# A sandwich block on one core: mean-free Wo with its bias as a product, a maximum over two PSUM banks, and a bank ring by last use

## The reference

```
x = x + layernorm(attention(layernorm(x)))      # RoPE, causal softmax, ctx @ Wo + b_out
x = x + layernorm(ffn(layernorm(x)))
ffn: scores = sigmoid(xt @ w_router.T); the two best, weights divided by their sum
     silu(xt @ wg.T) * (xt @ wu.T) @ wd.T of each chosen expert, weighted and summed,
     plus the same of both shared experts
layernorm(x) = (x - mean) / sqrt(var + 1e-5)     # over the last axis, no scale, no shift
```

## Time and profile before

| | us |
|---|---|
| median of 3 runs | 760.34 (759.79 to 762.09) |
| the profiled execution | 760.28 |
| its span, first to last instruction | 757.8 |
| PE busy | 705.5 (93%) |
| DVE busy | 605.7 (80%) |
| ACT busy | 431.8 (57%) |

### The profile page before, as it was taken

One profiled execution on the slowest core, in us unless ns is written; L12 is line 12 of the kernel. 1 busy time (PEld: TensorE's weight loads), 2 busy tenths in 40 slices (PEclk: granted clock), 3 DMA queues, 4 the chain that ended last, 5 costly groups with the idle time before them and its releaser, 6 DMA issues. The chain is left out here.

```text
span 757.8 us, 15818 instructions
## 1 busy us (share of the span) xinstructions
PE 705.5 (93%) x6002; PEld 564.7 (75%) x6002; DVE 605.7 (80%) x1364; ACT 431.8 (57%) x729; POOL 314.7 (42%) x444
## 2 busy tenths in 40 slices
PE   4779999999999998979998999999999999999994
PEld 2335555555555555768888999999999999988884
DVE  4998999999998885565866888888878878738885
ACT  2436765666667576334244777777776777632230
POOL 4113354454444455100223455445445543048854
PEclk9989999999999999989999999999999999999998
DMA  8000000000000000000124676776667676513311
GB/s 278 1 3 4 4 3 10 16 10 11 10 11 10 16 11 15 15 8 1 43 91 174 208 236 217 223 236 216 239 217 233 221 215 202 163 56 90 91 57 55
DMA packets 29131, 74.31 MB, mean 98 GB/s; under 512 B 4609, under 2 KB 18305, under 8 KB 29057
## 3 DMA queue, kind: packets, MB, share of 16 engines
q0 software_dynamic: 12208, 55.45, 22.6%
q1 hardware_dynamic: 16432, 17.20, 6.9%
q10 hardware_dynamic: 416, 0.66, 0.3%
HBM read 62.68 MB, written 10.22 MB: 96 GB/s over the span
## 5 line engine op out<-in xcount | busy, mean ns | idle before, releaser
L984 DVE TENSOR_TENSOR HF<-SS,PS 128x256 f32<-128x256 f32 (+1 forms) x155 | 75.9, 490 | 98.2 <-ACT SS L732 57.0
L732 ACT ACTIVATE SS<-PS 128x256 f32<-128x256 f32 (+1 forms) x155 | 68.2, 440 | 116.7 <-PE PS L396 112.2
L396 PE MATMUL PS<-XGH,WH 128*128 128x256 f32 x460 | 129.6, 282 | 2.8 <-DVE WL L1084 2.8
L396 PE MATMUL PS<-XGL,WH 128*128 128x256 f32 x460 | 129.3, 281 | 0.0
L396 PE MATMUL PS<-XGH,WL 128*128 128x256 f32 x460 | 129.3, 281 | 0.0
L821 DVE TENSOR_REDUCE NM<-PS 128x2 f32<-128x512 f32 (+1 forms) x192 | 122.6, 682 | 7.6 <-PE PS L396 6.6
L1084 DVE TENSOR_TENSOR WL<-RAW,WH 128x768 fp32r<-128x768 f32 x125 | 120.2, 963 | 3.5 <-ACT WH L659 2.8
L396 PE MATMUL PS<-WH,HH 128*128 128x256 f32 x390 | 112.4, 288 | 0.9 <-DVE ACC L995 0.8
L659 ACT ACTIVATE HH<-HF 128x256 fp32r<-128x256 f32 (+1 forms) x155 | 72.1, 465 | 71.4 <-DVE HF L984 64.1
L396 PE MATMUL PS<-WL,HH 128*128 128x256 f32 x390 | 110.4, 283 | 0.0
L396 PE MATMUL PS<-WH,HL 128*128 128x256 f32 x390 | 110.4, 283 | 0.0
(11 more groups left out here) (167 smaller groups left out, 1460.2 us busy)
## 6 DMA issues: line engine op xcount, KB each, us to landing
ys<-YO SPq DMA_DIRECT2D x23, 256.0 KB
RAW<-in_wsh SPq DMA_DIRECT2D x4, 768.0 KB, 6.5
X<-in_x SPq DMA_DIRECT2D x8, 256.0 KB, 5.3
xn<-YY SPq DMA_DIRECT2D x16, 128.0 KB, 1.7
out<-X SPq DMA_DIRECT2D x16, 128.0 KB
QT<-NMT SPq DMA_DIRECT2D x96, 4.0 KB
RAW<-in_wsh SPq DMA_DIRECT2D x2, 384.0 KB, 6.1
XG<-xn,XIDX POOLq DMA_INDIRECT x46
```

What stands on the lines that cost most here:

```text
L396: return eng.matmul(o, l, r, start=start, stop=stop, skip_group_check=True)
L732: t = eng.activation(SS[:, i % 2, 0:n], bank(b, 0, n), ACT.Silu)
L984: eng.tensor_tensor(HF[:, c % 2, 0:n], SS[:, c % 2, 0:n], bank(b, 512 - n, 512) if n == 256 else bank(b), ALU.mult).then_inc(free[b], 1)
```

## The change

It has these parts.

- **Mean-free Wo.** `prepare` (seven stages in steps 1 to 7) takes the mean of each row off Wo and the mean off the bias, on DVE, so that the product has mean zero over its 256 columns, and splits the bias in three bf16 parts, which SP copies to three partitions (three DMAs of 512 bytes). `b_out` adds the bias by one more matmul (three rows of ones against the three parts); ACT instead of DVE then takes the sum out of PSUM to YY; `b_norm` is gone and `b_add` multiplies by 1/deviation and adds in one instruction.
- **A maximum over two banks.** `late(k)` takes two neighbouring banks, and one reduce of 1024 elements takes the maxima of both. PE signals it with `laid`, and DVE signals both banks with one semaphore, `n_m`.
- **Ring by last use.** A single user gets the bank of 3 to 6 that was dealt out longest ago. The pair gets the two neighbours whose later-dealt one was dealt out longest ago.
- **RoPE** multiplies by the sine table in one instruction with the halves read in reverse order, instead of two.
- **K copies.** The two copies of K for the two row halves of PE are written by the same instructions (four instead of six: copy of 384, difference, copy of 256, difference of 128; the copy of 512 is gone).
- **Router in 16 columns.** The high and low parts of the router weights stand side by side, four matmuls of 16 columns instead of eight of 8, and the first stage of `pick` adds the two halves for 14 (then 2) tiles.
- **Places.** f_rope, b_stats and b_dev move two quarters later; b_add, b_stats2, b_dev2, b_norm2, b_turn2 and b_route 1 to 3 quarters earlier; the split of b_turn2 on DVE becomes a stage of its own, `b_low`, two quarters behind it.

```diff
-FRONT = [("f_stats", -101), ("f_dev", -97), ("f_norm", -90), ("f_turn", -85), ("f_qkv", -77), ("f_rope", -77),
+FRONT = [("f_stats", -101), ("f_dev", -97), ("f_norm", -90), ("f_turn", -85), ("f_qkv", -77), ("f_rope", -75),
          ("f_first", -69), ("f_second", -67), ("f_third", -65), ("q0", -53), ("q1", -56), ("k", -49)]
-BACK = [("b_turn", 47), ("b_out", 51), ("b_stats", 51), ("b_dev", 51), ("b_norm", 56), ("b_add", 59),
-        ("b_stats2", 59), ("b_dev2", 59), ("b_norm2", 66), ("b_turn2", 71), ("b_route", 75)]
+BACK = [("b_turn", 47), ("b_out", 51), ("b_stats", 53), ("b_dev", 53), ("b_add", 58),
+        ("b_stats2", 58), ("b_dev2", 58), ("b_norm2", 63), ("b_turn2", 68), ("b_low", 70), ("b_route", 73)]
 ORDER = "a 2 s0 d s1 b s2 v m0 t w m1 m2 m3 s3"
...
-                out.extend(("late", k, a) for k in firsts for a in range(2))
+                out.extend(("late", k) for k in firsts)
...
-        if n == 0:
-            out.append(("router_split", 0))
+        if 1 <= n < 8:
+            out.append(("prepare", n - 1))
...
+    use, after, lates, pair, count, ring = {}, {}, {}, {}, [0] * 8, [3, 4, 5, 6]
     for s in stages:
         if s[0] == "ring":
-            ring = s[1]
+            ring = list(s[1])
...
+            n = 2 if s[0] == "late" else 1
+            b = min((b for b in ring if b + n - 1 in ring), key=lambda b: max(ring.index(b + m) for m in range(n)))
+            wide = max(pair.get(b + m, 0) for m in range(n))
+            for m in range(n):
+                ring.remove(b + m)
+                ring.append(b + m)
+            if n == 2:
+                lates[s[1]] = (b, count[b], count[b + 1], wide)
+                pair[b] = pair[b + 1] = s[1] + 1
+            else:
+                count[b] += 1
+                use[s] = (b, count[b])
+                after[s] = wide
...
-                cs = [take(("late", k, a)) for a in range(2)]
+                c, f0, f1, m = lates[k]
+                cs = (c, c + 1)
+                e.wait_ge(free[c], f0)
+                e.wait_ge(free[c + 1], f1)
+                e.wait_ge(n_m, m)
...
                 for j in range(2):
                     for a in range(2):
                         t = mm(bank(cs[a], 256 * j, 256 * j + 256), heads(k, a, 128, 256)[:, j, :], side(k, a, 0, 256), False)
                         if j:
-                            t.then_inc(full[cs[a]], 1)
+                            t.then_inc(laid, 1)
...
                 elif what == "b_out":
                     read(e, ("b_turn", i))
-                    e.wait_ge(d_wo, 16)
+                    e.wait_ge(wo_c, 2)
+                    e.wait_ge(d_b3, 48)
                     c = take(s)
+                    mm(bank(c, 0, 256), ones3[:, :], B3[:, :], True, False)
                     for k in range(2):
-                        t = mm(bank(c, 0, 256), CTT[:, i % 2, 128 * k:128 * k + 128], WO[:, k, :], k == 0, k == 1)
+                        t = mm(bank(c, 0, 256), CTT[:, i % 2, 128 * k:128 * k + 128], WO[:, k, :], False, k == 1)
                     t.then_inc(full[c], 1)
...
+                        for a in (XH, XL):
+                            t = mm(bank(c, 0, 16), a[:, k, 128 * i:128 * i + 128], WRX[:, k, :, :].rearrange("p a e -> p (a e)"),
+                                   k == 0 and a is XH, k == 1 and a is XL)
                     t.then_inc(full[c], 1)
...
+                elif what == "b_out":
+                    made(e, s)
+                    made(e, ("b_turn2", i - 2))
+                    e.wait_ge(d_xn[i % 2], 16 * (i // 2))
+                    copy(YY[:, i % 2, :], bank(c, 0, 256)).then_inc(free[c], 1)
...
-                    copy(ES[:, i, :], bank(c, 0, 8)).then_inc(free[c], 1)
+                    copy(EW[:, i, :], bank(c, 0, 16)).then_inc(free[c], 1)
...
-                eng.tensor_tensor(RA[:, T, :].rearrange("p (h d) -> p h d", d=8), qk, C, ALU.mult)
-                eng.tensor_tensor(rb[:, :, 0:4], qk[:, :, 4:8], S[:, :, 0:4], ALU.mult)
-                eng.tensor_tensor(rb[:, :, 4:8], qk[:, :, 0:4], S[:, :, 4:8], ALU.mult).then_inc(r_a, 1)
+                eng.tensor_tensor(RA[:, T, :].rearrange("p (h d) -> p h d", d=8), r[:, 0:320].rearrange("p (h d) -> p h d", d=8), C, ALU.mult)
+                eng.tensor_tensor(rb, qk[:, :, ::-1, :], S, ALU.mult).then_inc(r_a, 1)
...
-                eng.tensor_copy(K[:, :, 0:4:3, :], R[:, 32:40, :].unsqueeze(2).broadcast_to([P, 8, 2, 8]))
-                eng.tensor_copy(K[:, :, 5, :], R[:, 32:40, :]).then_inc(k_1, 1)
+                eng.tensor_copy(K[:, :, :, 1:6:2, :], R[:, 32:40, :].unsqueeze(2).unsqueeze(3).broadcast_to([P, 8, 2, 3, 8])).then_inc(k_1, 1)
                 e.wait_ge(q_1, i + 1)
                 eng.tensor_tensor(Rt[:, 0:32, :], R[:, 0:32, :], Q[:, :, 0, :], ALU.subtract).then_inc(q_2, 1)
                 e.wait_ge(k_1, i + 1)
-                eng.tensor_tensor(Rt[:, 32:40, :], R[:, 32:40, :], K[:, :, 0, :], ALU.subtract).then_inc(k_2, 1)
...
-                eng.tensor_copy(K[:, :, 1:5:3, :], Rt[:, 32:40, :].unsqueeze(2).broadcast_to([P, 8, 2, 8])).then_inc(k_3, 1)
+                eng.tensor_copy(K[:, :, :, 2:5:2, :], Rt[:, 32:40, :].unsqueeze(2).unsqueeze(3).broadcast_to([P, 8, 2, 2, 8])).then_inc(k_3, 1)
                 e.wait_ge(q_3, i + 1)
                 eng.tensor_tensor(Q[:, :, 5, :], Rt[:, 0:32, :], Q[:, :, 3, :], ALU.subtract).then_inc(q_4, 1)
                 e.wait_ge(k_3, i + 1)
-                eng.tensor_tensor(K[:, :, 2, :], Rt[:, 32:40, :], K[:, :, 1, :], ALU.subtract).then_inc(k_4, 1)
-                e.wait_ge(k_4, i + 1)
-                eng.tensor_copy(KC[:, T, :, 1, :], KC[:, T, :, 0, :]).then_inc(k_5, 1)
...
+                eng.tensor_tensor(K[:, :, :, 0, :], Rt[:, 32:40, :].unsqueeze(2).broadcast_to([P, 8, 2, 8]), K[:, :, :, 2, :],
+                                  ALU.subtract).then_inc(k_4, 1)
...
+                o = NM[:, h, part, 4 * q:4 * q + 4]
                 e.wait_ge(n_1, k // 4 - 1)
-                if key[0] == "early":
-                    o, i = NM[:, h, 0, 4 * q:4 * q + 4], bank(c).rearrange("p (h t) -> p h t", t=128)
+                if part == 0:
+                    c = use["early", k][0]
+                    made(e, ("early", k))
+                    eng.tensor_reduce(o, bank(c).rearrange("p (h t) -> p h t", t=128), AXX, ALU.max, negate=True).then_inc(free[c], 1)
                 else:
-                    o = NM[:, h, 1, 4 * q:4 * q + 4].rearrange("p (j a) -> p j a", a=2)[:, :, key[2]]
-                    i = bank(c).rearrange("p (j t) -> p j t", j=2)
-                eng.tensor_reduce(o, i, AXX, ALU.max, negate=True).then_inc(free[c], 1)
+                    c = lates[k][0]
+                    e.wait_ge(laid, 2 * k + 2)
+                    eng.tensor_reduce(o.rearrange("p (j a) -> p a j", a=2), bank(c, 0, 1024).rearrange("p (a j t) -> p a j t", a=2, j=2),
+                                      AXX, ALU.max, negate=True).then_inc(n_m, 1)
...
+            def prepare(k):
+
+                if k < 3:
+                    e.wait_ge(d_bo if k == 2 else d_wo, 16)
+                    src = BO if k == 2 else WO[:, k, :]
+                    eng.bn_stats(BN[:, 48 + k, :], src[:, :]).then_inc(wo_s, 1)
+                    e.wait_ge(wo_s, 2 * k + 1)
+                    eng.bn_aggr(MV[:, 48 + k, :], BN[:, 48 + k, :]).then_inc(wo_s, 1)
+                    e.wait_ge(wo_s, 2 * k + 2)
+                    eng.tensor_scalar(src[:, :], src[:, :], MV[:, 48 + k, 0:1], None, ALU.subtract, ALU.bypass).then_inc(wo_c, 1)
+                elif k == 3:
+                    e.wait_ge(wo_c, 3)
+                    eng.tensor_copy(BB[:, 0, :], BO[0:1, :]).then_inc(wo_c, 1)
+                    e.wait_ge(wo_c, 4)
+                    eng.tensor_tensor(BR[:, 0, :], BO[0:1, :], BB[:, 0, :], ALU.subtract).then_inc(wo_c, 1)
+                elif k == 4:
...
+                if k == 0:
+                    for t in range(t0, t0 + n):
+                        read(e, ("b_route", t))
+                    t = eng.tensor_tensor(ES[:, t0:t0 + n, :], EW[:, t0:t0 + n, 0:8], EW[:, t0:t0 + n, 8:16], ALU.add)
...
-                elif what == "b_out":
-                    c, k = use[s]
-                    made(e, s)
-                    e.wait_ge(d_bo, 16)
-                    made(e, ("b_turn2", i - 2))
-                    e.wait_ge(d_xn[i % 2], 16 * (i // 2))
-                    eng.tensor_tensor(YY[:, i % 2, :], bank(c, 0, 256), BO[:, :], ALU.add).then_inc(free[c], 1)
...
-                elif what == "b_norm":
+                elif what == "b_add":
                     e.wait_ge(b_rs, i + 1)
-                    normed(YY[:, i % 2, :], YY[:, i % 2, :], 16 + i).then_inc(b_yn, 1)
-                elif what == "b_add":
-                    e.wait_ge(b_yn, i + 1)
-                    eng.tensor_tensor(X1[:, i, :], X1[:, i, :], YY[:, i % 2, :], ALU.add).then_inc(b_x1, 1)
```

(13 more changed lines are left out.)

107 lines of the change are left out of this document (54 added, 53 removed).

## The result

The changed kernel takes 798.56 us (median of 4 runs, 797.65 to 801.02) against 760.07 of the kernel before: ratio 1.0506, 95% interval 1.0475 to 1.0537. The profiled execution is the slowest of the four (801.02 us); its span is 799.3 us, 41.5 more than before.

What follows compares the result with a forecast made beforehand. In attention's steps 12 to 43 DVE and PE were both taken as nearly full, so their mutual waits count. Terms 13.4 + 3.6 + 3.6 − 4.5 = +16.1 on a 757.8 us span gave 776.5 us, range 760 to 794.

Steps and rivals of the forecast that it cites:

- the turn of 18.83 us: Steps 12 to 43 of attention: four steps would take 18.83 us instead of 17.16.
- the clock, left out of the sum: Rival: PE's new waits in attention lower its clock, giving 804 us, or 790 if in half the turns; chance 0.09.
- the cover of 1.86 us is gone. DVE waits 1.28 us: Second `early` of a turn: DVE work ahead of its reduce moves behind it, so DVE waits 1.28 us for PE.
- hidden in the waits: PE's added bias matmul, less four of b_route: below 0.4 us a turn either way, counted as nothing.
- b_stats and b_dev (0.56) and f_rope (0.76): DVE's work after the second `early` reduce, 0.56 and 0.76 us, with RoPE's single sine product at 0.38.
- The waits of 0.94 and 0.90 us: DVE waits 0.94 us because the `early` mask needs b_low, then 0.90 because `late` shares that `early`'s bank.
- +1.67, 8 times, 13.4 us: Steps 12 to 43: each of eight turns grows by 1.67 us, after 3.12 of waits and 1.29 saved; 13.4 in all.
- Steps 44 to 59, "+3.6": Steps 44 to 55: `late` on its own `early`'s bank in two of four steps, 1.2 us three times, +3.6.
- Prepare, "+3.6": Steps 1 to 7: the added DVE work of `prepare` taken in full, +3.6 us.
- The start of the experts, −4.5: PE's wait for tile 15's b_norm2 shortens, −2.4 us, and half clock behind it partly comes back, −2.1.
- The reduce: DVE's merged reduce of 1024 elements takes 1.13 us instead of 1.20, saving 4.5 us over 64.
- DVE's savings come through: Rival: PE fills the second `early` before DVE needs it, so all DVE savings count: 744.5 us, chance 0.13.

Runs made afterwards that it cites:

- e1_cover: Changed kernel with b_stats, b_dev and f_rope put back to their old places: 771.97 us, ratio 1.0167 to the kernel before.
- e9_nomask: Changed kernel with POOL's zeroing of masked exponentials cut to one column of 128 per block: 784.41 us, ratio 1.0331.
- e8_oldring: Changed kernel, all places as changed, but `late` in two single banks of a round-robin ring with two reduces: 782.42 us, ratio 1.0286.
- e2_banks: Changed kernel with b_turn2 and b_low moved to 71 and b_route to 75, to free the shared banks: 778.54 us, ratio 1.0255.
- e10_nomask_before: Kernel before with POOL's zeroing of masked exponentials cut to one column of 128 per block: 755.74 us, ratio 0.9944.
- e4_wide_before: Kernel before with only the reduce over two banks and the ring by last use added: 765.76 us, ratio 1.0087.
- e5_savings: Changed kernel with old places, RoPE's sine product in two instructions, `late` in two single round-robin banks with two reduces: 755.14 us, ratio 0.9949.
- e11_best: Same kernel as e5_savings, plus the changed places of BACK for the last batch only: 751.46 us, ratio 0.9886.
- e3_allback: Changed kernel with all places as before and RoPE's sine product in two instructions; two-bank reduce and ring stay: 766.04 us, ratio 1.0087.
- e6_rope2: Changed kernel with only RoPE's sine product back in two instructions: 798.47 us, ratio 1.0493.
- e7_again: Changed kernel loaded again, nothing changed: 787.58 us, ratio 1.0364 to the kernel before.
- e12_tail: Kernel before with only the places of BACK for the last batch changed: 754.40 us, ratio 0.9931.

## Why the prediction was wrong, step by step

The direction and its cause were right, the size was not: 776.5 was forecast, in 760 to 794, and 798.56 came. The same kernel loaded again took 787.58, inside that range but 11 us above the forecast. In the first profile the span grew by 41.5 us where the sum of the prediction has 16.1. The 25.4 us between them are these: 12.1 from the stall (480.2 against 468.1 us from step 60 on), 12.5 from steps 12 to 43, of which 6.3 are half clock and the rest turns that are longer at full clock, 1.6 from steps 44 to 59, 1.2 from the start of the experts, less 2.0 in the start and steps 0 to 11. So two things of the prediction failed: **the turn of 18.83 us**, which is 19.69 at full clock, and **the clock, left out of the sum**. The stall, which carried the time over the edge of the range, was in no step, and its cause stays open. By the steps:

- **"the cover of 1.86 us is gone. DVE waits 1.28 us"**: right, shown by e1_cover; 1.83 us, because PE's run has 0.22 us more (the bias matmul, which I put at nothing behind "hidden in the waits") and DVE came sooner.
- **"b_stats and b_dev (0.56) and f_rope (0.76)"** is the step that failed in the sum of a turn. The sine product takes 0.85 from start to start, not 0.38. I took the row of the old place, where POOL beside it works on single elements, for a place where it zeroes 512. e9_nomask shows 0.44 us of this in each turn and in PE's wait. POOL's timeline in the kernel before, beside the two sine products at 151.68 and 151.91 us:

```profile
151.47 0.37 POOL L1145 TENSOR_SCALAR VE<-MV 128x1 f32<-128x1 f32 x1 [2.77 <-DVE MV L1053]
151.93 0.73 POOL L1147 TENSOR_TENSOR RS<-VE,mhalf 128x1 f32<-128x1 f32 x1
```

- **The waits of 0.94 and 0.90 us** for b_low and for `late` on its own `early`'s bank: 0.84 and 0.92, right in size. The front laid the shared bank beside the ring; e8_oldring has it too, with the same waits, so it comes from the places. Freeing it (e2_banks) gave back only half of the waits.
- **"+1.67, 8 times, 13.4 us"**: a turn at full clock is 19.69 us, +2.53. Of the 0.86 missed, 0.44 is POOL's and 0.22 the bias matmul; the rest, 0.2, is spread over small differences.
- **The clock**, the rival with a chance of 0.09, came in half of the turns: in the profile three of the eight are 21.3 us instead of 19.7, and a fourth 21.1. The place was right, the price not: behind a wait of 2.08 us a stretch of half clock costs 1.6 us, not 3.4; that PE is not on the path all the time would explain it, and is argued. I had weighed the row of 94 to 231 us against it, in which PE's pauses are 0.43 us and less but for a single one of 1.43, and which says nothing of a pause of 2 us in each turn. The rule of the Trainium skill that I cited there ("TensorE: Matmul & The Clock Gate", section "A second HAM failure mode: psum-queue depth-cycling") fits these turns: PEclk 0.84 in 176.80 to 198.10 us.

The trace of before had the nearer case, ahead of that row: a wait of 2.35 us, behind which the granted clock fell to 0.52. PE's timeline, and then the window 57.70 to 60.00 us, of the kernel before:

```profile
56.27 0.39 PE L396 MATMUL PS<-CB 128*128 128x512 bf16 x1 [2.35 <-DVE NM L821]
```

```profile
57.70:60.00 2.30, 2.30 (x26) 0.86 (x23) 1.75 (x4) 1.94 (x2) 1.21 (x2) 0.52 0.02 5
```

What PE's longest repeated wait was, and the clock in steps 12 to 43, over the kernels run:

| kernel | wait of PE, us | PEclk | steps 12 to 43, us |
|---|---|---|---|
| e10_nomask_before | 0.29 | 1.00 | 134.0 |
| before | 0.41 | 1.00 | 136.9 |
| e4_wide_before | 0.63 | 0.99 | 141.8 |
| e5_savings | 0.76 | 1.00 | 134.8 |
| e11_best | 0.76 | 0.99 | 136.3 |
| e1_cover | 0.86 | 0.99 | 147.5 |
| e3_allback | 1.25 | 1.00 | 143.3 |
| e9_nomask | 1.65 | 0.96 | 155.4 |
| e2_banks | 1.66 | 0.97 | 154.8 |
| changed | 2.08 | 0.93 | 162.8 |
| e8_oldring | 2.14 | 0.86 | 165.6 |
| e6_rope2 | 2.58 | 0.86 | 171.9 |

Up to 1.25 us at most one of the eight turns is at a lower clock, from 1.65 on two or more are; within each group the order is rough (2.08 and 2.14 us lie far apart in the clock). That the wait is the cause is argued from it and not shown, for no run filled the wait with other matmuls. Why the same wait of 2.08 us is followed by half clock in every other turn stays open.

- **Steps 44 to 59, "+3.6"**: +5.2. **Prepare, "+3.6"**: steps 0 to 11 took 4.2 longer, but began 2.6 sooner, so half of it came; in e7_again they took 2.7 longer. No run took `prepare` out, and two profiles with the same attention differ by 1.6 us here (44.8 and 46.4 us in the kernel before and e12_tail), so this term is not measured.
- **The start of the experts, −4.5**: −3.3 in e7_again (471.4 to 468.1 us from step 60 on), where a wait of 1.77 us that was not there before stands beside the shortened one; alone in the kernel before it gave 4.5 us.
- **The reduce**, 1.13 us from start to start: right (164.88 to 166.01). Its saving is worth nothing here: it frees both banks at its end, and e4_wide_before is slower by 0.9%. In the prediction this was half a sentence, 0.80 against 1.33 us.
- **"DVE's savings come through"**: wrong as a rival too. Even with the places and the reduce undone (e5_savings) they give 4 us, and 7.5 with the places of the last batch (e11_best), not 16; more than half of what DVE was spared in a turn went into instructions that got longer beside POOL's zeroing.
- The stall at 716 us, 11 us in the medians, was in no step; the same program loaded again does not have it.
